# PSUM banks given in two fixed rings instead of by a planner, with more zero-weight matmuls at the start and a later last transposition

## The reference

```python
x = x + attention_a(layernorm(x), Wq, Wk, Wv)            # 16 heads of 8; softmax over all keys,
                                                         # then the causal mask on the probabilities
x = x + ffn(layernorm(x), router_w, expert_bias, ...)    # 8 experts of 128, top 2, and a shared one
x = x + attention_b(layernorm(x), w_qkv, w_out, b_out)   # rotary embedding, softmax, output projection
x = x + ffn(layernorm(x), router_w, expert_bias, ...)    # same weights again
```

## Time and profile before

| | us |
|---|---|
| median of three runs | 1748.45 |
| lowest, highest | 1739.39, 1748.89 |
| profiled execution, its own time | 1754.32 |
| its span | 1752.6 |

### The profile page before, as it was taken

One profiled execution on the slowest core, in us unless ns is written; L12 is line 12 of the kernel. 1 busy time (PEld: TensorE's weight loads), 2 busy tenths in 40 slices (PEclk: granted clock), 3 DMA queues, 4 the chain that ended last, 5 costly groups with the idle time before them and its releaser, 6 DMA issues.

```text
span 1752.6 us, 44428 instructions
## 1 busy us (share of the span) xinstructions
PE 1710.3 (98%) x16824; PEld 866.0 (49%) x16824; DVE 1527.3 (87%) x2895; ACT 1420.8 (81%) x2840; POOL 945.8 (54%) x1397
## 2 busy tenths in 40 slices
PE   7999999999999999999999999999999999999988
PEld 3444444555545555455554545445454455555557
DVE  7888888998989989899889999889998989999727
ACT  2688887898878888688886998879997889999862
POOL 5254444566966678476772546535544364555530
PEclk7799998999989999899999999989997999999999
DMA  5211111000101001010110102010110001100000
GB/s 171 89 55 63 69 57 51 21 21 20 57 2 56 21 20 56 12 47 21 32 45 2 38 20 74 20 38 2 45 33 13 2 13 34 38 8 2 8 7 13
DMA packets 39124, 61.13 MB, mean 35 GB/s; under 512 B 5568, under 2 KB 20544, under 8 KB 38784
## 3 DMA queue, kind: packets, MB, share of 16 engines
q1 hardware_dynamic: 38880, 58.28, 10.2%
q10 hardware_dynamic: 32, 0.01, 0.0%
HBM read 29.96 MB, written 27.26 MB: 33 GB/s over the span
## 4 chain that ended last, share of the span: by engine, by line
PE 89%; DVE 6%; ACT 2%; issue 1%; POOL 1%; SPq 1%; DMA 0%; ACTq 0%; DVEq 0%; POOLq 0%
PE ps_sum L1358 29%; PE ps_banks L1324 25%; PE ps_banks L1378 13%; PE ps_banks L1399 8%; PE ps_banks L1299 4%; DVE negmax L1096 3%; PE ps_banks L1259 2%; PE ps_banks L1313 2%; PE ps_banks L1245 1%; PE ps_banks L1266 1%; PE ps_banks L1369 1%; ACT probs L908 1%; SPq L623 1%; PE ps_banks L1281 1%; PE ps_sum L1337 1%
## 5 line engine op out<-in xcount | busy, mean ns | idle before, releaser
L1096 DVE TENSOR_REDUCE negmax<-ps_banks 128x1 f32<-128x512 f32 x2048 | 1296.0, 684 | 151.7 <-PE ps_banks L1299 131.9
L908 ACT ACTIVATE probs<-ps_banks 128x512 f32<-128x512 f32 x2048 | 1099.9, 610 | 184.6 <-PE ps_banks L1324 176.0
L1299 PE MATMUL ps_banks<-kx,qx 24*128 24x512 f32 x2048 | 603.7, 512 | 6.9 <-DVE negmax L1096 2.4
L1324 PE MATMUL ps_banks<-qx,kx 26*128 26x512 f32 x2048 | 557.2, 508 | 5.8 <-ACT probs L908 3.6
L1358 PE MATMUL ps_sum<-probs,vg 128*9 128x256 f32 (+1 forms) x6144 | 425.8, 381 | 2.0 <-ACT sums L915 1.3
L1324 PEld LDWEIGHTS ps_banks<-qx,kx 26*128 26x128 f32 x2048 | 214.6, 186 | 381.5 <-ACT probs L908 129.4
L781 POOL TENSOR_TENSOR hid<-hid,first 128x512 f32<-128x512 f32 x124 | 158.2, 1276 | 210.2 <-DVE hid L1123 123.6
L1299 PEld LDWEIGHTS ps_banks<-kx,qx 24*128 24x128 f32 x2048 | 243.1, 187 | 38.9 <-DVE negmax L1096 17.6
L793 POOL TENSOR_SCALAR scaled<-scaled,gates 128x128 f32<-128x128 f32 x496 | 175.2, 371 | 80.5 <-ACT scaled L965 79.9
L755 POOL TENSOR_TENSOR pdiag<-probs,causal 128x512 f32<-128x512 f32 x128 | 163.3, 1279 | 98.9 <-ACT probs L908 64.4
L1358 PEld LDWEIGHTS ps_sum<-probs,vg 128*9 128x9 f32 x6144 | 129.0, 90 | 163.2 <-issue 71.3
(11 more groups left out here) (121 smaller groups left out, 1383.6 us busy)
## 6 DMA issues: line engine op xcount, KB each, us to landing
qk_rows<-limbs SPq DMA_DIRECT2D x36, 512.0 KB, 3.7
qx<-qk_rows SPq DMA_DIRECT2D x124, 96.0 KB
kx<-qk_rows SPq DMA_DIRECT2D x124, 96.0 KB
qx<-mlimbs SPq DMA_DIRECT2D x508, 2.0 KB
qk_rows<-prod_c SPq DMA_DIRECT2D x8, 512.0 KB, 3.4
qk_rows<-prod_s SPq DMA_DIRECT2D x4, 512.0 KB, 3.0
out_dram<-x SPq DMA_DIRECT2D x8, 256.0 KB, 2.5
x<-in_x SPq DMA_DIRECT2D x3, 512.0 KB, 6.0
```

The lines of the kernel that those rows point to most:

```text
L908: act.activation(m.probs[:, blk % PROB_SLOTS, EXP_HEADS[k], :], bank, ACT.Exp, scale=SCALE).then_inc(s.freed[SCALAR], 1)
L1096: dve.tensor_reduce(m.negmax[:, unit // UNITS % 2, half, col:col + 1], bank, AX.X, ALU.max, negate=True).then_inc(s.freed[VECTOR], 1)
L1299: pe.matmul(bank_of(("scores", unit, k)), m.qx[rows, n % SLOTS, tile * P:(tile + 1) * P], m.kx[rows, n % SLOTS, half * CHUNK:(half + 1) * ...
L1324: pe.matmul(bank, m.kx[rows, n % SLOTS, j * P:(j + 1) * P], m.qx[rows, n % SLOTS, half * CHUNK:(half + 1) * CHUNK], start=True, stop=True) ...
```

## The change

Four edits. (1) `give_banks` no longer models costs. The score fills take banks 0, 1, 2 in turn, everything else takes 3, 4, 5, 6 in turn, in the order of the plan. (2) In the lead, after every second step from the 14th, one item `warm` is added: six of them. (3) `warm` is four zero-weight matmuls instead of two, there and in the first four steps. (4) In the tail the attention output keeps its places; the transposition `turn` moves from before unit 4 to before unit 6, `logits` from 6 to 7, the three parts of the chain from 7, 8, 9 to 8, 9, 10. The first expert that needs its gates is mixed at unit 11.

```diff
+WARM_FROM = 14
...
-READ_AFTER = 90
-WEIGHT = {"exp": (11, 49), "scores": (11, 60), "h1": (85, 100), "h3": (85, 0), "y": (95, 50), "mix": (95, 90),
...
-OTHER_WORK = {"weigh": (55, 0, 0), "copy": (0, 50, 0), "high": (0, 107, 0), "stats": (0, 0, 120), "moments": (0, 0, 60),
...
+RINGS = {"scores": 0}
+RING_BANKS = (0, 1, 2), (3, 4, 5, 6)
...
         else:
-            items.append(("warm", blk, part))
+            items.append(("warm",))
...
     for unit in range(LEAD):
         plan += side.get(unit, []) + scores_of(unit)
+        if unit >= WARM_FROM and unit % 2 == 0:
+            plan.append(("warm",))
...
-    assert late > 2
-    stages = [[("oturn", c)], [("omix", c), ("oadd", c)], [("stats", 3, c), ("moments", 3, c), ("apply", 3, c)],
-              [("turn", 3, c)], [("logits", 3, c)],
-              *([("chain", 3, c, 1, k) for k in range(CHAIN) if k // PART == part] for part in range(-(-CHAIN // PART)))]
-    side = {}
-    for i, stage in enumerate(stages):
-        add_side(side, {1 + i * (late - 1) // len(stages): stage})
+    assert late > 10
+    side = staged(1, (0, ("oturn", c)), (1, ("omix", c)), (1, ("oadd", c)),
+                  (2, ("stats", 3, c)), (2, ("moments", 3, c)), (2, ("apply", 3, c)), (5, ("turn", 3, c)), (6, ("logits", 3, c)),
+                  *((late - 4 + k // PART, ("chain", 3, c, 1, k)) for k in range(CHAIN)))
...
-        tensor, busy, bank_of = 0, {SCALAR: 0, VECTOR: 0}, {}
-        free, holder = [0] * BANKS, [None] * BANKS
+        last, given = {}, [0] * len(RING_BANKS)
         for item in plan:
             if item[0] in READER:
-                bank = min(range(BANKS), key=lambda k: free[k])
-                self.banks[item], self.holders[item] = bank, holder[bank]
...
+                ring = RINGS.get(item[0], len(RING_BANKS) - 1)
+                bank = RING_BANKS[ring][given[ring] % len(RING_BANKS[ring])]
+                given[ring] += 1
+                self.banks[item], self.holders[item] = bank, last.get(bank)
+                last[bank] = item
...
-    def warm(blk, part):
+    def warm():
         pe.wait_ge(s.acc_cleared, 1)
-        for t in range(2):
+        for t in range(CT):
             pe.matmul(m.acc[:, t * P:(t + 1) * P], m.zeros[:, :], m.ident[:, :], start=True, stop=True,
                       skip_group_check=True)
```

More of the change, by code:

```diff
@@ L68 @@
 READ_BY = {"product": "h3", "write": "direct"}
-READ_AFTER = 90
-WEIGHT = {"exp": (11, 49), "scores": (11, 60), "h1": (85, 100), "h3": (85, 0), "y": (95, 50), "mix": (95, 90),
-          "turn": (50, 80), "q": (95, 100), "k": (95, 100), "v": (95, 100), "direct": (190, 70), "qk": (95, 69), "logits": (95, 20),
-          "oturn": (50, 50), "omix": (100, 50), "maxima": (20, 25), "sums": (55, 50)}
-OTHER_WORK = {"weigh": (55, 0, 0), "copy": (0, 50, 0), "high": (0, 107, 0), "stats": (0, 0, 120), "moments": (0, 0, 60),
-              "combine": (0, 0, 33), "finish": (0, 0, 25), "chain": (0, 0, 20), "product": (0, 0, 69), "write": (0, 0, 70)}
+RINGS = {"scores": 0}
+RING_BANKS = (0, 1, 2), (3, 4, 5, 6)
 class Buffers:
@@ L1436, in tensor_program @@
         elif kind == "warm":
-            warm(*of)
+            warm()
         elif kind == "fill":
```

## The result

| | before | changed |
|---|---|---|
| median us | 1745.73 (4 runs, 1739.39 to 1748.89) | 1790.44 (4 runs, 1784.21 to 1796.95) |
| ratio, 95% interval | | 1.0248 [1.0219, 1.0276] |
| profiled execution's span | 1752.6 | 1782.3 |

The change makes the kernel 2.5% slower. 1747 was forecast, with a range from 1735 to 1760 for itself and up to 1776 with the rivals: the time lies above both.

What follows compares the result with a forecast made beforehand. VectorE was taken to pace plain steps and TensorE those with feed-forward, coupled by PSUM banks. Body +4, lead with zero-weight matmuls -1, tail -5: -2, 1752 against 1754.3 profiled, 1747 as median; range 1735 to 1760, with rivals 1720 to 1776.

Steps and rivals of the forecast that it cites:

- Three banks in the lead, +7.3: Lead: three score banks leave VectorE idle at half-clock projections, moving the first exponent from 45.49 to about 52.8 us.
- I take it that it holds: Lead and first steps: zero-weight matmuls keep the clock full; lead and zero-weight matmuls together -1 us, otherwise +11.
- Rival C: Lead: the clock doesn't hold, +11 there, +10 us in all, 1758 us; chance 0.12.
- The body, +4: Body, 54 to 1690 us: relief of 55 us and new waits of 62 us, discounted alike, leave +4 us.
- I take the difference at half to full: Body: the difference between 55 us of relief and 62 us of new waits, taken at half to full, gives +4 us.
- usable ends (+30): Body: the range given around the +4 us estimate, from -25 to +30 us.
- Where the new waits would lie: Body: new waits of over 1 us found at 124, 190 and 223 us, in the stretch without clock drops.
- Rival B: Body: three banks starve VectorE where TensorE has over about 1.2 us of other work; +29 us, 1777; chance 0.15.
- Rival D: Body: the rings bring five more clock drops in stretches without feed-forward, +24 us, 1771 us; chance 0.08.
- The tail, -5: Last turn: the transposition placed two units later no longer waits 4.01 us; -5 us, ends -6 and 0.
- The first steps, -8.7: Steps 0 to 8: at full clock they take about 12 us instead of 20.7, -8.7 us.
- The signs named to look for: Trace after: spread nearer 60 than 91 us, VectorE's score wait 110 to 150, full clock from about 32, no transposition stall.

Runs made afterwards that it cites:

- rings_only: The kernel before with only the new give_banks (rings of three and four banks); ratio to before 1.0250, first exponent at 60.5 us.
- no_lead_warm: The changed kernel without its six zero-weight items in the lead; ratio to before 1.0205, first exponent at 61.3 us.
- tail_only: The kernel before with only the later last transposition, router and chain; ratio to before 0.9951, last part 61.3 us instead of 67.1.
- body_rings: The changed kernel with the old planner giving banks before the first exponent and rings from there on; ratio to before 1.0136.
- planner_warm_tail: The changed kernel with the old planner's give_banks and weights put back; ratio to before 0.9916, repeated at 0.9928.
- warm_only: The kernel before with only the change's zero-weight matmuls (six items in the lead, four matmuls per item); ratio to before 0.9969.
- ring7: The changed kernel with one ring of all seven banks for every kind; ratio to before 1.0086.
- ring43: The changed kernel with four banks in turn for the scores and three for all else; ratio to before 1.0797.

## Why the prediction was wrong

- **Three banks in the lead, +7.3.** Wrong in size: +14 to +15 (60.5 in rings_only and 61.3 in no_lead_warm, against 46.3 and 45.5). The cycle was worked out with 1.5 us of starvation for four projections, which is 6 and not the 5 that went into the sum. rings_only shows eight waits of 1.16 to 1.82 us, 12.7 in sum, with three banks and half clock throughout the lead; at the same clock the planner's banks leave none above 0.6 (tail_only). I had taken over from one execution of before a clock that rises at about 31 us.
- **"I take it that it holds".** The step that failed first. The clock did not hold: after 18 us it did not rise until 76. With the same zero-weight matmuls and up to seven banks it rose at 30 to 41 us (body_rings, both executions of planner_warm_tail, warm_only, ring7), with four banks at 49 (ring43). What kept it down stays open. The stall of 0.78 us ahead of the fourth score of each cycle goes with it, but ring43 stood at 0.50 for 30.7 us without any stall. What it cost is shown: the six items of the lead, which the forecast had hidden at full clock, came to 9.4 us (70.7 less 61.3). Rival C, the clock that doesn't hold, had this step right and priced it at +11, 7.3 for the banks and 4 for the first steps; it left the lead's own six items out. Lead and first eight steps together: forecast -1, rival C +11, measured +20.2.
- **The body, +4.** The step that failed is "I take the difference at half to full": reliefs (55 us) and new waits (62 us), both laid over the old trace, were netted to nearly nothing. The runs show 26 to 29 us at equal clock, close to the upper of the usable ends (+30). By the comparison step by step the new waits came out nearly whole (54 us), the relief to less than half (25 us). In the stretch that carries feed-forward the planner's spreads were only 2.7 us in all, so there was little to relieve where TensorE is the bound.
- **Where the new waits would lie.** I looked at the large ones in the stretch without feed-forward. There 132 steps (8 to 140) take 201.4 instead of 197.7 us. Rival B, by which VectorE runs dry, is what happens in the lead. In the body its place, a stretch of TensorE work of over 1.2 us, was right, its engine was not: ahead of y VectorE does not run dry, TensorE is held ahead of y by a VectorE that has the product in front of the read.
- **Rival D**, more drops of the clock: not seen. The change had fewer microseconds at half clock in the body than before, and ring bodies (44 to 82) cover the same range as planner bodies (41 to 85). The section of the Trainium skill named with it ("TensorE: Matmul & The Clock Gate", section "A second HAM failure mode: psum-queue depth-cycling") has the clock swing between its levels. No trace here bears it out for the rings: in the body no swings were added, and in the lead, with three banks in turn and a stall of 0.78 us in each cycle, the granted clock stood at 0.50 without a swing.
- **The tail, -5**: right, -5.3 in the change and -5.8 alone (tail_only). The transposition comes with no idle time before it:

```profile
1741.04 1.05 PE L1382 MATMUL ps_banks<-w,hid 128*128 128x128 f32 x8
1741.92 0.60 PE L1228 MATMUL ps_banks<-ident,xn 128*128 128x128 f32 x4
```

- **The first steps, -8.7**: -5.0; the first two still ran at half clock. At full clock all the way they took 12.5 in ring7, as worked out, but 15.2 in planner_warm_tail and warm_only; what makes these 2.7 us was not taken apart.
- **The signs named to look for**: VectorE's wait for scores (136.3, within 110 to 150) and the stalled transposition came as said; the spread within steps rose to 131.6 instead of falling towards 60, and half clock still stood at 50 us. Those two were the wrong ones.

## What to carry to other kernels

When a bank or buffer plan is changed, lay the new plan over the old trace as here, but do not net relief against new waits over the whole span: here 54 of 62 us of new waits came, and 25 of 55 us of relief. Take the stretch where one engine is the bound, and count the new waits ahead of its long work in full. A small fixed ring fails where the reader has another task ahead of the read; a planner that knows that task avoids it, and one exchange at that place gave back 11.5 of 26 us. Work added to keep the clock up must be priced at the lower level until traces show that the clock rises (one trace is not enough: the same lead had 7 us of full clock in one execution and none in another), and it is only free if the engine that it covers has stock enough.

## What the runs showed that I had not expected

- With a wait of 0.78 us in each cycle of 4.3 us the lead of the change stayed at the lower level for 58 us (18 to 76); with the banks given by the planner and the same zero-weight matmuls the scores ran at full clock from 39 us. The bank plan is the only difference, but the wait itself is not shown to be the cause: ring43, without it, stood at 0.50 until 49 us, and so did tail_only, with the planner's banks and no zero-weight items in the lead, until 66.
- The lead of one and the same program differs by execution: first exponent 50.2 and 45.8 in planner_warm_tail and its repetition, where the clock rose at 39 and at 30 us, steps 0 to 8 15.2 and 18.0. Both sums, 65.4 and 63.8, lie within 2 us.
- A microsecond at half clock cost 0.28 us of body between the ends; held step by step against executions at full clock, the planner's seven bodies give 0.22 to 0.29. The earlier trace rows gives 0.28 too (2.0 against 1.43 us a step), but partly by luck: the stage at half clock carries some feed-forward (line 1378, 2.2 us) and the other none.
